# Keys, queries and both MLP layers of two attention passes by high and low parts

## What is computed

```python
x = _L0_conv_ref(x, ...)   # layernorm, linear, depthwise convolution over 3 tokens, gelu, linear, residual
x = _L1_conv_ref(x, ...)   # shifted 7 x 7 window attention and MLP
x = _L2_conv_ref(x, ...)   # norm, 7 x 7 depthwise convolution, window attention with bias and mask
x = _L3_conv_ref(x, ...)   # as the second, other weights
```

```python
q, k, v = jnp.moveaxis(qkv, 2, 0)
attn = softmax(einsum('wqhd,wkhd->whqk', q, k) * scale)
x = shortcut + project(attn @ v)
h2 = _ln(x, g2, b2)
mlp = gelu(h2 @ w_fc1 + b_fc1) @ w_fc2 + b_fc2
return x + mlp
```

## Time and profile before

| | us |
|---|---|
| median of the runs | 12334.83 |
| profiled execution | 12346.31, span 12344.5, mean granted TensorE clock 0.978 |
| TensorE busy | 11557.4 (94%) |
| DVE, ACT busy | 7030.2 (57%), 7537.9 (61%) |
| POOL busy | 1543.8 (13%) |
| second pass (span 2187 to 5977) | 3790.0, granted clock 0.97 |
| fourth pass (span 8640 to 12344.5) | 3704.5, granted clock 0.99 |

### The profile page before, as it was taken

One profiled execution on the slowest core, in us unless ns is written; L12 is line 12 of the kernel. 1 busy time (PEld: TensorE's weight loads), 2 busy tenths in 40 slices (PEclk: granted clock), 3 DMA queues, 4 the chain that ended last, 5 costly groups with the idle time before them and its releaser, 6 DMA issues. The chain is left out here.

```text
span 12344.5 us, 381409 instructions
## 1 busy us (share of the span) xinstructions
PE 11557.4 (94%) x153876; PEld 7528.1 (61%) x153876; DVE 7030.2 (57%) x12108; ACT 7537.9 (61%) x12498; POOL 1543.8 (13%) x2308
## 2 busy tenths in 40 slices
PE   6999998899999999999998999998999999999999
PEld 3434443566666666666675667666666666666666
DVE  4444444556556555555446666666555555555555
ACT  4555554566566566566435777776666666666666
POOL 0000000222222222222000000000111111111111
PEclk9999999899999999999999999999999999999999
DMA  1111111122222222222463333333000000000000
GB/s 56 37 36 39 40 39 34 37 46 46 45 45 46 46 44 47 44 47 45 153 216 69 76 75 76 75 75 66 21 21 21 21 21 21 22 21 21 22 21 20
DMA packets 1104420, 602.40 MB, mean 49 GB/s; under 512 B 864651, under 2 KB 1076566, under 8 KB 1099704
## 3 DMA queue, kind: packets, MB, share of 16 engines
q1 hardware_dynamic: 1091496, 553.66, 19.0%
q10 hardware_dynamic: 12288, 38.54, 0.9%
HBM read 308.38 MB, written 282.75 MB: 48 GB/s over the span
## 5 line engine op out<-in xcount | busy, mean ns | idle before, releaser
L950 PEld LDWEIGHTS banks<-L_ident,L_PR 113*113 113x113 f32 x9216 | 1104.5, 180 | 415.6 <-issue 290.1
L1264 DVE COPY L_VB<-banks 49x384 f32<-49x384 f32 x512 | 287.3, 561 | 1859.4 <-PE banks L966 1859.4
L1026 PE MATMUL banks<-L_XN,L_W 97*128 97x392 f32 x3072 | 1249.0, 516 | 13.2 <-DVE L_XN L1339 0.7
L1185 ACT ACTIVATE L_PR<-L_SX 113x588 f32<-113x588 f32 x1536 | 1084.3, 706 | 277.0 <-DVE L_SX L1301 270.5
L950 PE MATMUL banks<-L_ident,L_PR 113*113 113x113 f32 x9216 | 1249.1, 272 | 2.5 <-ACT L_PR L1185 1.8
L1295 DVE TENSOR_REDUCE L_MX<-banks 113x12 f32<-113x588 f32 x1024 | 783.4, 765 | 605.3 <-PE banks L988 605.3
L1169 ACT COPY L_PT<-banks 113x452 f32<-113x452 f32 x1792 | 871.1, 528 | 395.3 <-PE banks L950 395.2
L378 PE MATMUL banks<-scan_XS,scan_W1T 97*96 (+1 forms) x2688 | 1110.2, 551 | 0.0
L1103 PE MATMUL banks<-L_Hd,L_W 128*97 128x392 f32 x3072 | 1097.2, 493 | 0.0
L1005 PE MATMUL banks<-L_VB,L_PT 113*49 113x34 f32 x36864 | 1074.0, 214 | 2.5 <-ACT L_PT L1169 1.0
L1005 PEld LDWEIGHTS banks<-L_VB,L_PT 113*49 113x49 f32 x36864 | 1026.1, 127 | 26.9 <-issue 1.3
(11 more groups left out here) (199 smaller groups left out, 20433.5 us busy)
## 6 DMA issues: line engine op xcount, KB each, us to landing
L_X<-after_L SPq DMA_DIRECT2D x768, 147.0 KB
after_L<-L_X SPq DMA_DIRECT2D x512, 147.0 KB
conv_T<-L_norm_by_phase SPq DMA_DIRECT2D x96, 512.0 KB, 3.3
L_norm_by_phase<-L_XP SPq DMA_DIRECT2D x512, 84.0 KB, 2.2
scan_XT<-in_x SPq DMA_DIRECT2D x33, 1176.0 KB, 7.0
L_norm<-L_XA SPq DMA_DIRECT2D x256, 147.0 KB, 2.0
L_conv<-conv_D ACTq DMA_DIRECT2D x96, 392.0 KB, 3.0
L_XR<-L_norm SPq DMA_DIRECT2D x256, 147.0 KB, 2.2
```

The source lines that it names most:

```text
L950: mm = pe.transpose(bank(TURN[a])[0:SPAN, (k % 4) * SPAN:(k % 4 + 1) * SPAN], PR[:, st.v if lag else st.u, 2 * k:2 * k + 2, :].rearrange(" ...
L1026: pe.matmul(bank((7, 6, 7)[j])[:, 0:CH], W1[0:C + 1, j * 128:(j + 1) * 128], XN2[:, st.u], start=True, stop=True).then_inc(s[f"fc1_{j}"], 1)
L1185: act.activation(PR[:, u, a, 0:TOK], SX[:, u, a], ACT.Exp).then_inc(s[f"probs{half}"], 1)
```

## The change

In "L1" and "L3", keys, queries, all three hidden blocks and the three products of the second layer are computed from parts: `by_parts` issues three float32r matmuls where one f32 matmul stood. Weights are split once per pass by DVE (`split_weights`). Activations are split each step: XN by POOL (copy, then subtraction) for the next step's keys and queries; XN2 by ACT (copy) and DVE (subtraction) for the hidden blocks; the three gelu outputs by POOL. The second layer moves one step later (chunk t-3): blocks 0 and 1 stand after the queries, block 2 after `variances`. With it X2 moves to the front of DVE's step, the square of X2 and the third norm in "L1" one step later, and the last step of "L1" too (LAST 3 to 4). Queries take bank 3, X1 has four buffers in these passes. DVE's order becomes X2, `pt0`, keys, norms, values. The core of the diff:

```diff
+                def by_parts(out, wh, wl, xh, xl):
+                    for n, (wt, xt) in enumerate(((wh, xh), (wh, xl), (wl, xh))):
+                        mm = pe.matmul(out, wt.bitcast(F32R), xt.bitcast(F32R), start=(n == 0), stop=(n == 2))
+                    return mm
...
-                    pe.matmul(bank((7, 6, 7)[j])[:, 0:CH], W1[0:C + 1, j * 128:(j + 1) * 128], XN2[:, st.u],
-                              start=True, stop=True).then_inc(s[f"fc1_{j}"], 1)
+                    cols = slice(j * 128, (j + 1) * 128)
+                    by_parts(bank((7, 6, 7)[j])[:, 0:CH], W1H[0:C + 1, cols], W1L[0:C + 1, cols], XN2H[:, st.u], XN2L[:, st.u]).then_inc(s[f"fc1_{j}"], 1)
...
+                def output(st, j):
+                    st.wait(f"hd_parts_{j}", 3)
+                    for n, (wt, xt) in enumerate(((W2H, HdH), (W2H, HdL), (W2L, HdH))):
+                        mm = pe.matmul(bank(6)[0:C + 1, 0:CH], wt[:, j, :].bitcast(F32R), xt[:, st.v, j].bitcast(F32R),
+                                       start=(j == 0 and n == 0), stop=(j == HB - 1 and n == 2))
+                    return mm
...
                 def mlp_step(st):
-                        st.wait("xn", 0)
+                        st.wait("xn_parts", 0)
+                        st.wait("gelu_2", 3)
                         keys(st)
+                        st.wait("v_even", 1)
+                        st.wait("v_odd", 1)
+                        queries(st)
+                    if st.n:
+                        st.wait("gelu_1", 3)
+                        output(st, 0)
+                        output(st, 1)
                     if st.k:
                         st.wait("probs0", 1)
                         turn(st, 0)
-                    if st.f:
-                        if st.n:
-                            st.wait("x2", 3)
-                        queries(st)
                     if normed:
                         variances(st)
+                    if st.n:
+                        output(st, 2).then_inc(s["fc2"], 1)
...
-                    if st.m:
-                        for j in range(HB):
-                            mm = pe.matmul(bank(6)[0:C + 1, 0:CH], W2[:, j, :], Hd[:, st.u, j], start=(j == 0), stop=(j == HB - 1))
-                        mm.then_inc(s["fc2"], 1)
...
@@ mlp_step of DVE @@
+                    if st.n:
+                        st.wait("fc2", 3)
+                        dve.scalar_tensor_tensor(X2[:, st.v], bank(6)[0:C + 1, 0:CH], fc2b[:, 0:1], x1_of(st, 3), ALU.add, ALU.add).then_inc(s["x2"], 1)
+                    if st.k:
+                        pt_copy(st, 0)
                     if st.f:
                         keys(st)
-                    if st.k:
-                        pt_copy(st, 0)
...
@@ mlp_step of ACT @@
+                    if st.m:
+                        st.wait("xn2", 2)
+                        act.copy(XN2H[:, st.u].bitcast(F32R), XN2[:, st.u]).then_inc(s["xn2_high"], 1)
...
@@ POOL @@
+                    def split_rows(st):
+                        held(st, "xn", 0)
+                        pool.tensor_copy(XNH[:, st.u].bitcast(F32R), XN[:, st.u]).then_inc(s["xn_high"], 1)
+                        held(st, "xn_high", 0)
+                        pool.tensor_tensor(XNL[:, st.u].bitcast(F32R), XN[:, st.u], XNH[:, st.u], ALU.subtract).then_inc(s["xn_parts"], 1)
...
+                    def split_units(st, j, lag):
+                        u = st.v if lag % 2 else st.u
+                        st.wait("fc2", lag + 2)
+                        held(st, f"gelu_{j}", lag)
+                        pool.tensor_copy(HdH[:, u, j].bitcast(F32R), Hd[:, u, j]).then_inc(s[f"hd_high_{j}"], 1)
+                        held(st, f"hd_high_{j}", lag)
+                        pool.tensor_tensor(HdL[:, u, j].bitcast(F32R), Hd[:, u, j], HdH[:, u, j], ALU.subtract).then_inc(s[f"hd_parts_{j}"], 1)
```

## The result

The changed kernel takes 13128.8 us (median of three, 13101.2 to 13167.2) against 12334.8: a ratio of 1.064, 95% interval 1.061 to 1.068. The forecast was 12712, with 13050 as its upper end. The direction was right; 417 us are missing from the sum, and the time lies 79 us above its upper end.

What follows compares the result with a forecast made beforehand. TensorE, busy 94%, was taken to bound the kernel. Fourth pass +318 us, second +49, once +10: +377 on the profiled 12346.3, which lay 11.5 above the median, gave 12712 (chance 0.60), range 12400 to 13050.

Steps and rivals of the forecast that it cites:

- The second pass's return: Second pass's loop end: instructions fetched at every return, 6.2 us a round (3.1 idle, 0.6 second gap, 2.5 clock).
- The fourth pass's return: Fourth pass's loop end: loop no longer fits, fetched at every return, 6.2 us a round where nothing was fetched before.
- the second gap of 0.6: At a loop's return: a second TensorE idle, inside `variances` in the kernel before, stays at 0.6 us a round.
- the 2.5 for the clock: At a loop's return: lower clock after TensorE's idle costs 2.5 us a round, taken between 1.2 and 3.8.
- Products, 0.84 us a step: TensorE's step: three reduced-type records take 0.54 us for 0.66, gaining 0.12 seven times, 0.84 us a step.
- DVE's order, +0.57 us: Between `turn` 1 and `spread`: TensorE waits for DVE's `pt0` copy queued behind X2, 1.89 us for 1.32, +0.57 a step.
- POOL, 0.2 us in the second pass and none in the fourth: POOL's splits at 1.53 us form a ring: 13.3 us sets the second pass's step by 0.2; the fourth's equals TensorE's.
- rival C: POOL's splits cost 1.8 us, adding 3.2 us a round in the second pass, 2.4 in the fourth: 13060; chance 0.16.
- TensorE waiting for HdL on POOL by more than 0.3 us a step: Sign in TensorE's step that would show the forecast wrong and POOL's splits dearer, at 1.8 us.
- comes to 14.0, just TensorE's: Fourth pass: POOL's ring over the hidden blocks and three splits takes 14.0 us a step, the same as TensorE alone.
- Rival A: Fourth pass's loop code stays in place, no fetch at its return: 12328, no change, or 12250; chance 0.12.
- Rival B: Returns fetched but light, products at 0.165 us a record and clock's part at 1.2 us: 12450; chance 0.12.

Runs made afterwards that it cites:

- before_aligned: Kernel before with 22 small constant products ahead of the second pass, moving both loops' code by 88 instructions: 12261.6 us, ratio 0.995.
- after_wide: Changed kernel with variance and `spread` products 196 columns wide instead of 98, half as many, same arithmetic: 12882.6 us, ratio 1.045.
- after_pt0_first: Changed kernel with DVE's copy of the first turned block moved ahead of X2: 12404.7 us, ratio 1.007.
- pt0_wide: after_wide with DVE's copy of the first turned block moved ahead of X2: 12005.2 us, ratio 0.974.
- after_no_hidden_low: Changed kernel without POOL's subtractions for the hidden units' low parts, the high part multiplied twice instead: 12496.1 us, ratio 1.014.
- wide_no_hidden_low: after_wide without POOL's subtractions for the hidden units' low parts, the high part standing in: 12061.0 us, ratio 0.979.
- after_placed_pt0: Changed kernel with DVE's copy of the first turned block ahead of X2 and 59 and 47 small products ahead of the passes: 12786.4 us.
- before_placed: before_aligned with the fourth pass's loop shifted by 168 more instructions, 256 in all: 12106.4 us, ratio 0.983.

## Why the prediction was wrong, step by step

**The second pass's return, 6.2 us: wrong.** The step that failed is that the second pass's loop, at 1744 records where 1680 "doesn't fit", would be fetched at every return. It took the number of instructions for the cause. before_aligned shows that place and length decide together: the very loop whose fetching was the argument stays when moved by 88 instructions, and the other is then fetched. By the place that it happened to get, the longer second-pass loop stayed in most of its rounds, against the Trainium skill's memory as the prediction had applied it (Runtime: NRT & Kernel Launch, Instruction fetch mechanics), by which a longer loop had to be fetched too. Against the fetch-free after_wide the few fetches cost it 0.8 us a round, so this term was 5.4 too high, 330 us.

**The fourth pass's return, 6.2 us: fetched as forecast, 3.3 in size.** 66.26 against 62.97 in after_wide. The idle was right:

```profile
10074.85 0.61 PE L991 MATMUL banks<-L_XNH,L_WkH 97*96 97x392 f32 x1 [3.38 <-issue]
10075.25 0.53 PE L991 MATMUL banks<-L_XNL,L_WkH 97*96 97x392 f32 x1
10075.58 0.53 PE L991 MATMUL banks<-L_XNH,L_WkL 97*96 97x392 f32 x1
```

3.38 us here, 3.0 in the mean, forecast 3.1. What failed are the second gap of 0.6, which doesn't occur in this place, and the 2.5 for the clock: records are 0.33 apart behind the stop (10075.25, 10075.58) instead of 0.18, but stretches at half clock occur in these steps without a return too, so that it adds little to them. 2.9 a round too high, 177 us. The 2.5 wasn't wrong everywhere. With the fourth pass's loop in the same place, but the steps themselves at full clock, a return costs 4.2 us (61.44 in after_pt0_first against 57.19 in pt0_wide) and 5.4 (62.76 in after_no_hidden_low against 57.40 in wide_no_hidden_low), with the wide products' 0.1 in both. So the price hangs on what the steps around it do to the clock, and on the place besides: 2.4 in before_aligned, 6.4 in after_placed_pt0. No step of the prediction had either.

**Products, 0.84 us a step: 0.2.** The price of a record was right: three take 0.53 in the rows of wide_no_hidden_low. TensorE's own work fell by 0.67 us a step, short of 0.84 because a triple isn't 0.54 everywhere: the first record of a row after other work takes 0.23 to 0.29, and the four transposes ahead of hidden block 2 take 0.60 to its first record where it was 0.43. The larger part of the miss is that the gain doesn't arrive: the ring through POOL sets the step, and what TensorE gains it gives back waiting for HdL.

**DVE's order, +0.57 us: +0.68.** From `turn` 1 to `spread` it is 2.00 us (10045.59 to 10047.59) for 1.32. In the second pass it is 2.17 (2596.24 to 2598.41) for 1.31 (5038.30 to 5039.61), since X2 starts 0.37 us after `turn` 1 where the fourth pass, as the prediction had it, needs 0.20. The mechanism was right. With the copy moved ahead (pt0_wide) the step falls by 1.24 and 1.10 us, more than this stretch had grown: in the kernel before it held 0.27 of idle for RS.

**POOL, 0.2 us in the second pass and none in the fourth: about 1.05 a step.** The mechanism was right, a ring that sets the step, and its terms were too small. In the second pass it measures 14.41 for 13.3. From the end of DVE's XN (2585.45 + 0.55) to output block 2 (2595.63) it is 9.63 where the prediction had 8.9. The split of XN alone makes 0.54 of that, 2.07 for 1.53, as its cast takes 0.88; the three hidden splits are 1.66 to 1.70 from start to start. From output block 2 to the end of the next XN it is 4.78 for 4.4. With splits of 0.51 + 0.18 + 1.02 = 1.71 and 0.88 + 0.18 + 1.02 = 2.08 the mean of the four is 1.80, which is rival C's price. C's mechanism is what the second pass shows, and "TensorE waiting for HdL on POOL by more than 0.3 us a step" came true, at 0.7. That C's 13060 came near the result is luck all the same: its returns were 507 us too dear, and it had neither the clock in the steps nor the fourth pass's full loss. In the fourth pass the ring measures 15.4 for 14.0. The prediction gives no terms for that 14.0; the splits' price explains 0.4 of the miss and `turn` 1 to `spread` 0.1, and which term lacked the rest stays open. What is certain is the step that failed: "comes to 14.0, just TensorE's", by which POOL was to cost nothing there. The wait for PT lies in the same ring, so that neither of the two covers the other.

**The clock inside the steps: absent from the sum.** It was looked for at returns alone. It cost 3.0 us a round in the second pass (57.6 to 60.63) and 1.4 in the fourth, with three stops a step that come to 1.6 to 1.8 us. With the stop for PT alone (wide_no_hidden_low, 0.86 to 1.02) or those for HdL alone (pt0_wide, 0.75 to 0.79) it stayed at 1.00. That the stops cause the fall is shown by taking either away, with the same work in the steps; how the chip judges isn't.

Put together, in us over 61 rounds, measured less forecast: returns -330 (second pass) and -177 (fourth); steps 57.6 against 53.0 in the second pass, +281, and 61.6 against 56.0 in the fourth, +342; clock in the steps +185 and +84; once +28. That is +413. It is to be held against 406, the 783 us between the two profiled executions less the 377 forecast (the forecast counted 62 rounds for these 61). The other 11 of the 417 are those that the forecast took off because the kernel before's profile lay above its median; the changed kernel's does not.

Rival A decided on "whether q8 has packets in that loop": it has, so A was rightly low, though in the other pass the very thing it describes came true in most rounds. Rival B's return (4.9 us) was nearer than the forecast's and still too dear; its products at 0.165 weren't right. The range ended at 13050 "just short of C", and C is the rival that came, with a lower clock inside the steps that no case had.

Left open: by what rule a place decides. 256 instructions further is the same place. Loops of 1664 and 1680 records a round had places where they stayed and others where they didn't; those of 1488 to 1600 (the wide kernels) stayed in every place that they happened to have; for those of 1728 and 1744 no place was found in which they always stay.

## What to carry to other kernels

Look at the queue that brings instructions before and after a change that makes an unrolled loop longer: in these kernels some tens of small products ahead of the loop decided over 2 to 6 us a round, and half as many, wider products settled it. Price a stop of an engine that is otherwise full at more than its idle time (here by some 0.2 us), and look at the granted clock of single rounds: in these kernels the stop for PT alone, or those for HdL alone, left it at 1.00, and all three together did not. When work is moved to a half-empty engine, its load says little; follow the ring from where its input is made to where its output is wanted and on to the next input, with each instruction's price for the type that it writes, and put other work of the busy engine into that stretch.

## What the runs showed of the hardware

POOL's copy into the reduced type takes 0.51 us for 128 partitions of 392 elements, but XN's, with 97 partitions, 0.88 in nearly all cases, though 0.51 in the one at a pass's start when DVE stood still. In the timeline a DVE subtraction (L1401) runs beside it. The three lines, with ns as min/median/max, then first and last start:

```profile
L1467 POOL CAST L_XNH<-L_XN x512: 511/881/885, 2200.2 to 13057.0; 97x392 fp32r<-97x392 f32 x171
...
L1401 DVE TENSOR_TENSOR L_XN2L<-L_XN,L_XN2H x512: 566/568/569, 2233.1 to 13103.6; 97x392 fp32r<-97x392 f32 x171
...
L1469 POOL TENSOR_TENSOR L_XNL<-L_XN,L_XNH x512: 1009/1022/1044, 2200.8 to 13058.1; 97x392 fp32r<-97x392 f32 x171
```

That the two contend is argued from that and wasn't tried. The subtraction into the reduced type takes 1.02 us on POOL and 0.57 on DVE. The Trainium skill (GPSIMD Engine Reference, Engine selection) has POOL about twice as slow as VectorE for two inputs; the trace agrees, at 1.8 times, better than the earlier trace rows did.

That an instruction fetch in a program of one core depends on a shift of code far away, and can cost 1.7% of a kernel, I hadn't expected: before_placed is the kernel before in all but 64 small products.
